# A layernorm's reciprocal roots in two halves: GpSimd's power of one half of the tiles beside VectorE's work on the other

## The reference

```
def _layernorm(x, axis=-1, eps=1e-05):
    m = jnp.mean(x, axis=axis, keepdims=True)
    v = jnp.var(x, axis=axis, keepdims=True)
    return (x - m) / jnp.sqrt(v + eps)
...
    h = _layernorm(x, axis=-1) * (1 + ca) + sa
    x = x + ga * attention(h)
    h = _layernorm(x, axis=-1) * (1 + cb) + sb
    x = x + gb * feed_forward(h)
```

## Time and profile before

| | |
|---|---|
| Times of three runs | 5750.97, 5768.01, 5766.71 us (median 5766.71) |
| Profiled execution | 5765.86 us, its span 5764.1 us |
| TensorE busy | 4946.6 us (86%) |
| VectorE busy | 3368.9 us (58%) |
| ScalarE busy | 2579.5 us (45%) |
| GpSimd busy | 1321.8 us (23%) |
| L301, the layernorms' power | 8 instructions, 23.2 us together |
| L295, the rows | 128 instructions |

### The profile page before, as it was taken

One profiled execution on the slowest core, in us unless ns is written; L12 is line 12 of the kernel. 1 busy time (PEld: TensorE's weight loads), 2 busy tenths in 40 slices (PEclk: granted clock), 3 DMA queues, 4 the chain that ended last, 5 costly groups with the idle time before them and its releaser, 6 DMA issues. The chain is left out here.

```text
span 5764.1 us, 125494 instructions
## 1 busy us (share of the span) xinstructions
PE 4946.6 (86%) x50206; PEld 3467.1 (60%) x50206; DVE 3368.9 (58%) x6334; ACT 2579.5 (45%) x6938; POOL 1321.8 (23%) x1478
## 2 busy tenths in 40 slices
PE   5699998999989999899996998888887894599969
PEld 4477776777767776677775555555554453355545
DVE  4477676767767677676774666545543554443231
ACT  2355555555555555455553443444441334334521
POOL 0333333333333333333331000111101210012200
PEclk7799999999999999999997999999998797778879
DMA  2000000000000000000001001000000000000000
GB/s 86 23 20 23 16 18 21 20 24 19 15 21 24 20 19 15 21 23 20 19 20 48 1 1 62 7 1 0 1 21 14 15 1 13 23 1 1 1 22 15
DMA packets 51263, 106.13 MB, mean 18 GB/s; under 512 B 12848, under 2 KB 20176, under 8 KB 49520
## 3 DMA queue, kind: packets, MB, share of 16 engines
q1 hardware_dynamic: 50672, 98.07, 5.7%
HBM read 90.43 MB, written 5.52 MB: 17 GB/s over the span
## 5 line engine op out<-in xcount | busy, mean ns | idle before, releaser
L1076 DVE SCALAR_TENSOR_TENSOR dh_kq<-bank,dh_conv_kq,dh_kq 128x511 f32<-128x511 f32 (+2 forms) x408 | 305.2, 748 | 178.8 <-ACT dh_kq L892 167.6
L1076 DVE SCALAR_TENSOR_TENSOR dh_v<-bank,dh_conv_v,dh_v 128x511 f32<-128x511 f32 (+2 forms) x384 | 285.8, 748 | 169.4 <-ACT dh_v L892 159.3
L638 PE MATMUL bank<-hT,dh_w_kq 128*128 128x512 f32 x544 | 276.7, 633 | 49.9 <-DVE dh_kq L1076 42.4
L638 PE MATMUL bank<-hT,dh_w_vz 128*128 128x512 f32 x512 | 271.1, 656 | 51.0 <-DVE dh_v L1076 51.0
L1289 POOL TENSOR_TENSOR dh_pto<-dh_qkm,dh_et 128x512 f32<-128x512 f32 x128 | 160.6, 1276 | 649.8 <-PE bank L614 649.8
L1143 DVE TENSOR_TENSOR dh_turned<-dh_turned,bank 128x256 f32<-128x256 f32 x384 | 153.8, 414 | 249.7 <-ACT dh_turned L937 248.0
L1818 PE MATMUL bank<-moe_h_split,moe_w 128*128 128x512 bf16 x1200 | 277.3, 381 | 14.4 <-PEq L89 14.4
L808 PE MATMUL bank<-dh_wo_gated,dh_ww 128*128 128x256 f32 x1040 | 266.6, 414 | 0.8 <-ACT dh_ww L983 0.8
L301 POOL TENSOR_TENSOR ln_rstd<-ln_var_eps,nhalf 128x16 f32<-128x16 f32 x8 | 23.2, 2904 | 1047.4 <-DVE ln_var_eps L291 1047.4
L650 PE MATMUL bank<-dh_w_vz,hT 128*128 128x256 f32 x1024 | 245.5, 383 | 0.0
L808 PEld LDWEIGHTS bank<-dh_wo_gated,dh_ww 128*128 128x128 f32 x1040 | 210.0, 207 | 36.7 <-issue 1.1
(11 more groups left out here) (428 smaller groups left out, 12410.9 us busy)
## 6 DMA issues: line engine op xcount, KB each, us to landing
dh_rates<-delta_rates SPq DMA_DIRECT2D x130, 256.0 KB, 3.3
dh_w_vz<-in_L_wvz SPq DMA_DIRECT2D x17, 512.0 KB, 3.3
mod_w<-in_L_wmod SPq DMA_DIRECT2D x4, 1536.0 KB, 7.1
dh_w_kq<-in_L_wkq SPq DMA_DIRECT2D x18, 256.0 KB, 2.7
dh_wo<-in_L_wo SPq DMA_DIRECT2D x16, 256.0 KB, 4.4
moe_w<-in_L_w13T SPq DMA_DIRECT2D x1, 3200.0 KB, 16.4
later_gates<-mod_gate SPq DMA_DIRECT2D x3, 1024.0 KB, 4.0
gate<-later_gates SPq DMA_DIRECT2D x6, 512.0 KB, 3.4
```

The costliest lines, as they stand in the source:

```text
L638: last = pe.matmul(pj_bank(n), w[:, kk, :], k.hT[:, kk, n % NB, :], start=(kk == 0), stop=(kk == KD - 1))
L1076: dve.scalar_tensor_tensor(y, pj_bank(n)[:, 0:S - i], taps(n)[:, TAPS - 1 - i:TAPS - i], y, ALU.mult, ALU.add).then_inc(s["v_cs" if i < TA ...
```

## The change

The 16 tiles are treated as two halves of eight (two sequences each). VectorE takes statistics, aggregates and adds epsilon for the first half and then for the second; GpSimd computes two powers of 128x8, one for each half, each when its epsilon instruction has ended; the rows of the first half wait for the first power and those of the second for the second.

```diff
             def _(dve):
+                for h in range(2):
+                    tiles = range(h * NT // 2, (h + 1) * NT // 2)
+                    for t in tiles:
+                        dve.bn_stats(st[:, t, :], k.x[:, t // NC, t % NC, :]).then_inc(stats, 1)
+                    for t in tiles:
+                        dve.wait_ge(stats, t + 1)
+                        dve.bn_aggr(mv[:, t, :], st[:, t, :]).then_inc(aggr, 1)
+                    dve.wait_ge(aggr, (h + 1) * NT // 2)
+                    dve.tensor_scalar(ve[:, tiles.start:tiles.stop], mv[:, tiles.start:tiles.stop, 1], 1.0e-5, None,
+                                      ALU.add).then_inc(vare, 1)
                 for t in range(NT):
-                    dve.bn_stats(st[:, t, :], k.x[:, t // NC, t % NC, :]).then_inc(stats, 1)
-                for t in range(NT):
-                    dve.wait_ge(stats, t + 1)
-                    dve.bn_aggr(mv[:, t, :], st[:, t, :]).then_inc(aggr, 1)
-                dve.wait_ge(aggr, NT)
-                dve.tensor_scalar(ve[:, :], mv[:, :, 1], 1.0e-5, None, ALU.add).then_inc(vare, 1)
-                dve.wait_ge(rs, 1)
-                for t in range(NT):
+                    if t % (NT // 2) == 0:
+                        dve.wait_ge(rs, 1 + t // (NT // 2))
                     after(dve, turned, t - 3)
                     dve.tensor_scalar(xn[:, t % 4, :], k.x[:, t // NC, t % NC, :], mv[:, t, 0:1], rstd[:, t:t + 1],
                                       ALU.subtract, ALU.mult).then_inc(normed, 1)
...
             def _(pool):
-                pool.wait_ge(vare, 1)
-                pool.tensor_tensor(rstd[:, :], ve[:, :], k.nhalf[:, 0:NT], ALU.pow).then_inc(rs, 1)
+                for h in range(2):
+                    part = slice(h * NT // 2, (h + 1) * NT // 2)
+                    pool.wait_ge(vare, h + 1)
+                    pool.tensor_tensor(rstd[:, part], ve[:, part], k.nhalf[:, part], ALU.pow).then_inc(rs, 1)
                 if fill:
                     fill(pool)
```

## The result

The changed kernel takes 5729.99 us in the median of six runs (5724.04 to 5740.16), the kernel before 5763.0 us (5750.97 to 5769.75) in the runs beside them. The ratio is 0.9947 (95% interval 0.9931 to 0.9964): 0.53% faster, some 30 us by the ratio (the two medians differ by 33). I had forecast 5758.5 us with a range down to 5742. Even the rival in which the second power is hidden gave only 5747.

A forecast was written before the change was run, and what follows sets the result against it. The layernorms' path was taken to hold VectorE's 3.02 us wait for GpSimd's power; less 0.2 added and a 1.7 stall, 1.1 us per call, 7.8 in seven calls, giving 5758.5 us, range 5742 to 5768.

The forecast's parts named there:

- the rival in which the second power is hidden: In the layernorms the second power causes no stall: 2.8 us won per call, 19.7 in seven, 5747 us; chance 0.31.
- Term (d), the stall of the second power: Second half's power beside the first half's rows: a stall between 0 and 1.8 us, taken as 1.7 for each call.
- The claim that 24.2 us is the most that the change can win: VectorE's waits before the rows, 3.02 us in each of eight layernorms, limit any rearrangement's gain to 0.42%.
- the case with both powers exposed: Rival in the layernorms: neither power is hidden, 0.5 us slower for each call, 5770 us; chance 0.05.
- The epsilon and its wait: In each layernorm VectorE's additional epsilon and wait for aggregations add 0.2 us, between 0.1 and 0.3.
- A power of 128x8: GpSimd's power split in each layernorm: a half costs 1.67 us, not 1.45, because of a constant of about 0.4.
- The first power is hidden: First half's power, 1.67 + 0.1 us, fits beside the second half's statistics and aggregation, 3.3 us, without disturbance.
- ln10 gives nothing: After ln10 the next stage's first weight load is released by a DMA, about 7 us of slack; seven calls count.
- ln20 wins 3.1 us, like the others: In ln20 the memsets follow the second power and shut out remaining rows for the same 13.8 us; its sum is unchanged.

The follow-up runs named there:

- Experiment 7: The changed kernel with two more 128x8 powers into an unused tile behind the second one in each layernorm, beside the rows; ratio 0.9942.
- Experiment 9: The changed kernel, except that the first row waits for both powers; ratio 0.9971.
- experiments 1 to 6: Controls of both kernels (0.9998, 0.9947), split in first layernorm only (0.9979), split plus extra statistics (0.9987), two VectorE setup memsets (0.9988), one GpSimd memset (no ratio).
- experiment 10: The changed kernel with the split in all layernorms but the first, which stays as before; ratio 0.9974.
- experiment 8: The changed kernel with a GpSimd memset of 128x2048 into an unused tile right behind the second power in each layernorm; ratio 0.9987.
- experiment 5: The kernel before with two tiny VectorE memsets of an unused column added in the setup stage; ratio 0.9988.
- experiments 4: The changed kernel with eight more VectorE statistics instructions, results unused, ahead of the rows in each layernorm; ratio 0.9987.

## Why the prediction was wrong

*Term (d), the stall of the second power, failed.* I took 1.7 us from the rows shut out by products and memsets, and it is 0. The two bounds that I had (0 and 1.8) hold, and the row for the lower one was before me: products with two SBUF inputs ran unhindered beside a power. I gave more weight to the likeness of the VectorE instruction than to that of the GpSimd instruction, although it is the latter that does the shutting out. Experiment 7 shows that rows, which write to SBUF, run unhindered beside three powers in a row; so whatever a power holds, it doesn't keep the rows from it. Experiment 9 shows that the size of the stall would have been right, 1.76 us. This step is worth 1.7 us in each of seven calls, 12 us.

*The claim that 24.2 us is the most that the change can win, failed.* It counts the wait alone, and takes everything behind a barrier as moved and otherwise the same. Layer 0's attention became 9 to 10 us faster and the block attention 4, without a change in either. In both TensorE spends less time at half clock: 276.0 us instead of 293.5 in the first, 181.2 instead of 191.4 in the second. What VectorE's program holds ahead of the loop moves the first on the average (experiments 1 to 6 and 10), but by what way stays open. For the block attention I have no experiment: it takes 540.6 to 540.8 us in every kernel that leaves ln30 as it was, and in those that split it anything from 536.7 (experiment 10) to 541.3 (experiment 7) and 543.3 (experiment 8). This was in no rival, and with it the time fell below the hidden case and out of the range.

*The distance.* Between 5758.5 and 5729.99 us lie 28.5. The missing stall is 12 of them. Some 4 are the start: I counted from a median of 5766.71, and the kernel before took 5763.0 in the runs beside the changed one. The rest, some 13 us, is what the two attentions gave. Two sums of mine were off by little: 5758.1 and 0.85 are 5758.9, not 5758.5, and the case with both powers exposed is 0.67 us slower for each call by its own terms, not 0.5.

*What held.* The epsilon and its wait cost 0.23 us in ln00 (6.82 us from the first statistics to the second epsilon's end where 6.59 were needed before), against 0.2. A power of 128x8 takes 1.64 us, against 1.67. The first power is hidden: it disturbs no statistic (409 ns in the median, before and after). ln10 gives nothing: its next stage starts 26.9 us after its start, released by the DMA as before. ln20 wins 3.1 us, like the others, since its memsets follow the second power. The rival that the second power is hidden came true inside the layernorms: 19.7 us by its sum, and 19.9 and 20.1 in the two pairs of profiles. It had 0.31 of my chances, and for the whole time it too was 17 us too high.

The Trainium skill's rule on the shared pair of ports (page "SBUF — State Buffer", section "Who interferes with whom"), by which a GpSimd instruction keeps them for its whole length, agrees with the memset of experiment 8 (a row of 1890 ns beside 1.93 us of it). It doesn't agree with the powers: 1.90 and 3.35 us of them lay beside rows of at most 415 ns (experiment 7). The rule is for VectorE instructions in a two-port mode, and it is the memset's row that suggests that these are such.

## What to carry to other kernels

Before an instruction is hidden beside another, ask what the one that would do the blocking is: a small power beside these rows cost them nothing, a memset of 1.93 us made one of them 1.5 us longer. Look for a row of the trace in which that same instruction lies beside any instruction of the other engine, and give it more weight than a row in which only the other instruction is alike. Where a kernel has long loops, leave room in the range for what happens to code that isn't changed: two idle instructions ahead of this loop moved the whole by 7 us (2 to 12 by the interval). An edit of that size in gain should be tried once against a kernel that only shifts the program, as in experiment 5, before the gain is put down to the edit.

## What the runs showed of the hardware

- VectorE paused 0.35 us in front of an instruction whose inputs were ready, in each of four trips of a loop (idle for 5.70 us instead of 5.35), and the pause vanished when its program had two more instructions ahead; one more of GpSimd left it. What in VectorE does this stays open.
- After the same idle time of TensorE, 3.13 us, one kernel was granted 0.50 of the clock (1.2 GHz) and the other 1.00 (2.4). A mean granted clock of 0.97 instead of 0.98 goes with 1.7 us more in a stretch of 175. Over layer 0's attention, TensorE's busy time for the same matmuls differs by 8.8 of the 9.2 us.
- GpSimd's power gives way to a VectorE row for 0.26 us (1.90 us instead of 1.64) and then goes on beside the rows. Where VectorE runs statistics or waits instead, it takes 1.64 us (experiments 4 and 9).
- A GpSimd memset of 128x2048 (1.93 us) held one row for 1890 ns. Of two memsets with no wait between them, a row was held out by both (13.84 us, before), or a row got in between them (7.0 and 7.1 us, after).
